# Four graph layers on one core: the third layer's node update contracted in another order, the last layer's loop by eight turns

## The chip, the cores and the metric

The kernel runs on one core of a Trainium2 chip. The metric is the device time of one execution in microseconds (us), the median of several runs. Engines are named as in the profile: PE (TensorE), DVE (VectorE), ACT (ScalarE), POOL (GpSimd) and SP (SyncE, which here only issues DMAs).

## The reference

A network of four graph layers on 3125 nodes (D = 160 features each: CS = 64 scalars and CV = 32 vectors of 3 components) and 103125 edges, all in fp32. Two parts are touched.

The third layer's update: with `x` a node's features and `a` the sums over its edges,

```
u0 = einsum('nu,nv,uvw->nw', xs, a0, Wu_ss)/64 + einsum('nui,nvi,uvw->nw', xv, a1, Wu_vv)*c
u1 = einsum('nu,nvi,uvw->nwi', xs, a1, Wu_sv)*k + einsum('nui,nv,uvw->nwi', xv, a0, Wu_vs)*k
```

The last layer's attention: per edge a message is formed from two node rows, 64 logit features `a` come out of a matrix product, then

```
a = where(a > 0, a, 0.2*a);  a = sum(a * alpha_dot, axis=-1)     # per head, 4 heads of 16
alpha = softmax of a over the edges of a destination node
agg = segment_sum(alpha * h, dst)
```

where `h` is a second product of the same message. The softmax is kept running: a maximum per node is raised and the sums are shrunk as edges come in.

## The kernel before

Every stage is a block in which each engine runs its own program, written out by hand; engines meet through semaphores, and nothing reorders instructions. Within an engine the order of the code is the order of execution.

**The update (stage_layer2, last part).** Nodes are the columns: 10 turns `t` of W = 320 nodes, two turns to a loop iteration. A bilinear term needs the products of every pair `x_u * a_v`. DVE makes them (`prod`, 128x1280 each, L1902): one operand holds rows of `x` broadcast over 32 partitions (`xs4`, `xv4`), the other holds `a` (or `a1`) four times over the partitions. PE contracts each product with a slice of the weights into two PSUM tiles (`p_s`, `p_v`, L1998). A turn has 38 products: 12 for the family Wu_sv, 8 for Wu_ss, 12 for Wu_vs and 6 for Wu_vv. Nine `prod` buffers go round. SP loads the operands for the next turn when DVE has made the last product that reads the single buffer: `xs4` after its 20th product, `xv4` after its 38th. `xs4` and `xv4` are single; `a0` and `a1` are double. ACT loads the weights at the start with 26 DMAs, and DVE scales them before the first operand load may start.

**The last layer's loop (stage_layer3).** Edges are sorted by destination. A turn `u` takes a pair of 128-edge tiles; 428 pairs and three turns of draining give 432 turns, written out `TURN` = 4 to a loop iteration, so 108 iterations. Each of DVE and PE reads its node-block registers with one load at the head of an iteration (`reg_load`). A turn works on three pairs at once:

- for the pair ahead: PE turns one-hots and edge rows (`front_turn`), ACT copies them out of PSUM (`front`, L2480 and L2481, `front_copied`), PE makes the front rows (`front`, L2391 and L2393);
- for the pair `u`: DVE makes the message (L2591) and the first product F; PE turns F in the next turn, ACT copies it (L2509);
- for `prev`: PE makes logits and values (L2430, L2432, `logits_done`), ACT copies 64 logit features (L2518), takes tanh (L2519) and the gate (L2522); DVE applies the leaky rectifier (L2625), multiplies with alpha_dot (L2630) and sums (L2635); DVE makes the second product G;
- for `prev2`: PE turns G (L2444), ACT copies it to `g_t` (L2529), PE makes the heads (L2455, L2457, `heads_done`), DVE weights them (L2656 to L2663), PE sums them per node (L2470, `summed`), and DVE adds the sums (L2594).

DVE's L2596 takes the largest masked logit; PE's next masked product and then its logits wait for it.

## Time and profile before

| | us |
|---|---|
| median of 3 runs | 13256.09 (13255.51 to 13270.1) |
| the profiled execution | 13278.26, its span 13276.5 |
| update: first to last product | 8420.6 to 8955 of the span |
| last layer's loop: first to last message | 9118.5 to 13183.4 of the span |
| busy: PE, DVE, POOL, ACT | 72%, 67%, 57%, 34% of the span |

Times in the rows below are us from the span's start. The update and the loop together are 4600 us, a third of the span; the rest (sorting, the first layers' edges) isn't touched. Busy shares over the whole span mix stages with different limits, so each stage is read by itself.

### The profile page before, as it was taken

How to read it: one execution, taken by the hardware profiler on the slowest of the kernel's cores; microseconds unless marked ns; L12 is line 12 of the kernel's file. 1: busy time of each engine (PE TensorE's matmuls, PEld its weight loads, DVE VectorE, ACT ScalarE, POOL GpSimd, SP SyncE). 2: the span in 40 equal slices, each digit the busy share in tenths (PEclk: the TensorE clock that was granted, in tenths of full speed). 3: DMA queues.
4: the chain of work that ended last, by engine and by line, in shares of the span. 5: the costliest groups of instructions: out<-in, count | busy, mean ns of one | idle time of the engine just before them, and what ended most of it. 6: DMA issues, size and time to landing. Idle time of an engine off the chain costs nothing. (4 is left out here: it accounts for less than half of the span.)

```text
span 13276.5 us, 248283 instructions
## 1 busy us (share of the span) xinstructions
PE 9568.8 (72%) x62786; PEld 6478.2 (49%) x62787; DVE 8841.3 (67%) x26382; ACT 4480.1 (34%) x14978; POOL 7557.1 (57%) x12370
## 2 busy tenths in 40 slices
PE   4444545458888577677766777676888888888887
PEld 2111111136666444444444555335777777777776
DVE  6666766656666433333334555697889989989997
ACT  0000000025555211111112222004777677777775
POOL 2555556555555455555526666003777777777775
PEclk8666666668888777777767788897999999999998
DMA  4000000012222222222213333660000000000000
GB/s 129 22 22 23 23 20 24 17 34 58 58 58 57 54 55 55 55 55 55 55 34 87 81 81 73 115 126 20 21 21 22 21 21 21 21 21 22 21 21 22
DMA packets 901346, 597.92 MB, mean 45 GB/s; under 512 B 654301, under 2 KB 831283, under 8 KB 898584
## 3 DMA queue, kind: packets, MB, share of 16 engines
q0 software_dynamic: 235616, 359.73, 10.8%
q1 hardware_dynamic: 650712, 197.85, 8.3%
q10 hardware_dynamic: 14624, 35.51, 0.7%
q8 instruction: 196, 3.21, 0.1%
q14 instruction: 198, 1.62, 0.0%
HBM read 513.01 MB, written 79.56 MB: 45 GB/s over the span
## 5 line engine op out<-in xcount | busy, mean ns | idle before, releaser
L1290 POOL DMA_INDIRECT l1s_node_rows<-node_table,l1s_edge_rows x1216 | 1245.7, 1024 | 1160.4 <-DMA l1s_edge_rows<-rows_by_src 696.9
L2329 POOL DMA_INDIRECT l_source_rows<-node_table,l_edge_rows x866 | 854.3, 986 | 1102.0 <-DMA l_edge_rows<-rows_by_dst 841.8
L546 PE MATMUL rank<-onehots_and_before,lower_h 128*128 128x427 f16 x812 | 392.4, 483 | 1372.6 <-DVE onehots_and_before L494 651.0
L570 POOL DMA_INDIRECT rows_by_src<-row_s,pos_i x812 | 780.9, 962 | 951.8 <-DVE pos_i L506 686.6
L871 POOL DMA_INDIRECT l_source_rows<-node_table,l_edge_rows x880 | 871.7, 991 | 717.2 <-DMA l_edge_rows<-rows_by_dst 374.5
L1635 POOL DMA_INDIRECT l2s_node_rows<-node_table,l2s_edge_rows x864 | 863.4, 999 | 607.8 <-issue 251.2
L1401 ACT COPY l1s_outer<-l1s_p_outer 128x1024 f32<-128x1024 f32 x304 | 307.6, 1012 | 2053.9 <-remote 1561.0
L570 POOL DMA_INDIRECT rows_by_dst<-row_d,pos_i x812 | 785.1, 967 | 271.4 <-issue 270.5
L1321 DVE TENSOR_TENSOR l_sums_s<-l_sums_s,l1s_p_sums_s 128x8 f32 x1280 | 207.3, 162 | 1089.5 <-remote 688.1
L546 PEld LDWEIGHTS rank<-onehots_and_before,lower_h 128*128 128x128 f16 x812 | 83.2, 103 | 1629.8 <-issue 1121.5
L494 DVE TENSOR_REDUCE onehots_and_before<-onehots_and_before 128x427 f16<-128x2135 f16 x202 | 861.7, 4266 | 22.1 <-issue 20.0
L1375 PE MATMUL l1s_p_outer<-l1s_edge_by_node,l1s_node_rows 128*32 128x128 f32 x7296 | 620.4, 339 | 232.5 <-issue 228.1
L1372 PE MATMUL l1s_p_outer<-l1s_edge_by_node,l1s_node_rows 128*64 128x128 f32 x4864 | 530.1, 333 | 356.1 <-issue 272.1
L939 PE MATMUL l_p_sum<-l_messages,l_node_onehot 128*128 128x384 f32 x1728 | 691.9, 550 | 129.4 <-DVE l_messages L988 84.3
L1665 PE MATMUL l2s_p_sum<-l2s_rows_by_edge,l2s_node_onehot 128*128 128x352 f32 x1728 | 695.0, 520 | 113.8 <-issue 110.3
L548 PE MATMUL rank<-onehots_and_before,ones_h 128*128 128x427 f16 x2030 | 751.7, 484 | 0.0
L1692 DVE TENSOR_TENSOR l_sums<-l_sums,l2s_p_sum 128x512 f32 x440 | 301.2, 684 | 540.2 <-remote 475.1
L1372 PEld LDWEIGHTS l1s_p_outer<-l1s_edge_by_node,l1s_node_rows 128*64 128x64 f32 x4864 | 374.5, 167 | 547.4 <-issue 524.5
L1648 ACT ACTIVATE l2s_rows_by_edge<-l2s_node_rows,l2s_edge_rows 128x160 f32<-128x160 f32 x864 | 293.3, 415 | 1012.8 <-remote 746.2
L2457 PE MATMUL l_p_turn_heads_v<-l_w_hv,l_product_turned 128*128 128x128 f32 x3456 | 573.2, 288 | 0.0
L1375 PEld LDWEIGHTS l1s_p_outer<-l1s_edge_by_node,l1s_node_rows 128*32 128x32 f32 x7296 | 362.8, 132 | 427.5 <-issue 418.0
L1665 PE MATMUL l2s_p_sum<-l2s_node_rows,l2s_node_onehot 128*128 128x160 f32 x1728 | 379.1, 330 | 253.0 <-issue 218.7
(547 smaller groups left out, 29050.1 us busy)
## 6 DMA issues: line engine op xcount, KB each, us to landing
l_xv_by<-h_turned_l SPq DMA_DIRECT2D x120, 320.0 KB
l_source_rows<-node_table,l_edge_rows POOLq DMA_INDIRECT x1746
l_xs_by<-h_turned_l SPq DMA_DIRECT2D x40, 640.0 KB
l1s_edge_rows<-rows_by_src SPq DMA_DIRECT2D x1216, 19.5 KB
l1s_node_rows<-node_table,l1s_edge_rows POOLq DMA_INDIRECT x1216
rows_by_src<-pad_rows_s ACTq DMA_DIRECT2D x16, 1053.0 KB
l2s_edge_rows<-rows_by_src SPq DMA_DIRECT2D x216, 78.0 KB
l_edge_rows<-rows_by_dst SPq DMA_DIRECT2D x220, 72.0 KB
```

Source lines behind the costliest of these rows:

```text
L494: nc.vector.tensor_reduce(hots[:, (r + 1) % 4, SETS, :], hots[:, r, :, :].rearrange("p s b -> p b s"), AX.X, ALU.add).then_inc(counted, 1)
L548: nc.tensor.matmul(to, K["ones_h"][:, :], hots[:, r, m, :], start=False, stop=False)
L570: pool.indirect_dma_start(rows_, bass.IndirectOffsetOnAxis(ap=pos_i[:, k, o, t:t + 1].bitcast(U32), axis=0), tile[:, k, t, :], None).then_ ...
L871: pool.indirect_dma_start(xg[k][:, s, :], None, K["table0"], bass.IndirectOffsetOnAxis(ap=pay[k][:, s, D_SRC:D_SRC + 1].bitcast(U32), axis ...
L939: ins = nc.tensor.matmul(p_sum[:, h, 0:MW], hot[k][:, s, :], msg[k][:, s, :], start=s == PAIR * h, stop=s == PAIR * (h + 1) - 1)
L1290: pool.indirect_dma_start(xg[q][:, s, :], None, table, bass.IndirectOffsetOnAxis(ap=pay[q][:, s, S_DST:S_DST + 1].bitcast(U32), axis=0)).t ...
L1372: nc.tensor.matmul(p_o[rows, q % PO, s, col:col + n], lhs(xg[q][:, s, :]), rhs(eh[q % RING][:, s, :, :]), start=True, stop=True, skip_grou ...
L1375: ins = nc.tensor.matmul(p_o[rows, q % PO, s, col:col + n], lhs(xg[q][:, s, :]), rhs(eh[q % RING][:, s, :, :]), start=True, stop=True, ski ...
L1635: pool.indirect_dma_start(xg[k][:, s, :], None, table, bass.IndirectOffsetOnAxis(ap=pay[k][:, s, S_DST:S_DST + 1].bitcast(U32), axis=0)).t ...
L1665: ins = nc.tensor.matmul(p_sum[:, k % BANKS, h, cols], hot[r][:, s, :], rows[:, s, 0:cols.stop - cols.start], start=s == PAIR * h, stop=s ...
L2329: pool.indirect_dma_start(xg[u][:, s, :], None, K["table0"], bass.IndirectOffsetOnAxis(ap=pay[u][:, s, D_SRC:D_SRC + 1].bitcast(U32), axis ...
L2457: ins = nc.tensor.matmul(p_t[:, s, AT_HV:AT_HV + P], g_t[s][:, (c + 1) * P:(c + 2) * P], w_hv[:, c, :], start=c == 0, stop=c == 1)
```

## The change

**In the update**, the families Wu_sv and Wu_vs are contracted over one index first. For a slice of 16 output features, PE multiplies the weights, laid out by output, with `x` scalars (`hs`, 64 rows) or with `a` scalars (`as_`, a new load), into a PSUM tile `p_mapped` of four banks (`fill`, 4 matmuls, four times in a turn). DVE multiplies that PSUM tile with `a1` or with `x` vectors four times over the partitions (`xf`, a new load), and PE adds up rows with a constant 0/1 matrix (`pick`). The two families so need 6 products each where they needed 12. `p_mapped` is single: a fill waits for the last product that reads it, and the first product after it waits for the fill (`filled`). The order of groups, and with it the point at which SP may load, changes: `xs4` is last read by product 11 of 26, `xv4` by product 23 of 26. Weights come with 16 DMAs.

**In the last layer's loop**, `TURN` is 8, with rings of eight buffers for edge rows, source rows and one-hots (54 iterations of 8 turns). The rectifier is split: leaky(a) = 0.2 a + relu(0.8 a). The linear part comes out of the logits' product as 4 more columns of `w_a`, made beforehand; ACT makes relu(0.8 a) and copies the 4 columns, and DVE keeps one multiplication and one sum, over 17 instead of 16 columns per head. On ACT, the copies of one-hots and edge rows (`front`) stand behind the copies of the turned second product and the exponential.

```diff
-            for g in range(4):
-                groups.append(("v", [("xs4", "a1", lambda k, g=g, i=i: (xs4[:, KB * g:KB * (g + 1), :], a1[k][:, i, :])) for i in range(3)],
-                               [w_sv[:, KB * g + j, :] for j in range(KB)]))
...
+            def mapped(name, w, x, by, g):
+                fills[len(groups)] = [(w[:, KB * g * 4 + 4 * j:KB * g * 4 + 4 * (j + 1), :].rearrange("u w v -> u (w v)"), x) for j in range(KB)]
+                groups.append(("v", [("map", name, lambda k, i=i: (p_m[:, :, 0:W], by[k][:, i, :])) for i in range(3)],
+                               [pick[:, KB * g + j, :] for j in range(KB)]))
+            groups, fills = [], {}
+            of_scalars(0)
+            of_scalars(1)
+            mapped("a1", map_sv, hs, a1, 0)
+            of_scalars(2)
+            of_scalars(3)
+            mapped("a1", map_sv, hs, a1, 1)
+            of_vectors(0)
+            mapped("xf", map_vs, as_, xf, 0)
+            of_vectors(1)
+            mapped("xf", map_vs, as_, xf, 1)
...
+                    if m in fill_first:
+                        dve.wait_ge(filled, t * FILLS + (fill_first.index(m) + 1))
...
+                            sp.dma_start(as_[k][:, :], aT[0:CS, n]).then_inc(arrived_a["lin"][k], 16)
...
+                            for to, of, name in ((a1, aT, "a1"), (xf, hT, "xf")):
+                                for j in range(4):
+                                    sp.dma_start(to[k][j * SPAN:(j + 1) * SPAN, :, :], vectors(of)).then_inc(arrived_a[name][k], 16)
...
+                            def fill(f):
+                                last = first_of[order[f - 1]] + 3 if f else 0
+                                pe.wait_ge(made, t * OPS + (OPS + last))
+                                pe.sem_inc(seen, 1)
+                                for j, (w, x) in enumerate(fills[order[f]]):
+                                    ins = nc.tensor.matmul(p_m[:, j, 0:W], w, x[k][:, :], start=True, stop=True, skip_group_check=True)
+                                ins.then_inc(filled, 1)
...
-    TURN = 4
+    TURN = 8
...
-                            nc.scalar.copy(alphas[:, :, :], logits[:, :, 0:CS]).then_inc(m["alphas_made"], 1)
+                            nc.scalar.activation(alphas[:, :, :, 0:AS], logits[:, :, 0:CS].rearrange("p s (h c) -> p s h c", h=HEADS), ACT.Relu, scale=0.8)
+                            nc.scalar.copy(alphas[:, :, :, AS], logits[:, :, D:D + HEADS]).then_inc(m["alphas_made"], 1)
...
-                            wait("front_turned")
-                            wait("front_done", -1)
-                            front((u + 1) % 4)
                             wait("heads_done", -1)
...
                             nc.scalar.activation(Z[:, :, :, HW - 1], ea[:, :, :], ACT.Exp).then_inc(m["ex_done"], 1)
+                            wait("front_turned")
+                            wait("front_done", -1)
+                            front((u + 1) % TURN)
...
-                            wait("alphas_made")
-                            nc.vector.scalar_tensor_tensor(leaky[:, :, :], alphas[:, :, :], 0.2, alphas[:, :, :], ALU.mult, ALU.max).then_inc(m["leaky_made"], 1)
```

**Where instructions stand, update, PE, before.** The rows are one turn's matmuls into `p_upd_v` and `p_upd_s`; `l_outer` is a product of DVE, and a group of 12 belongs to three products.

```order
L1998 MATMUL l_p_upd_s<-l_h_scalars,l_l_s 64x320
L1998 MATMUL l_p_upd_v<-l_h_vectors,l_l_v 32x320 x3
L2006 REGISTER_ALU
L1998 MATMUL l_p_upd_v<-l_outer,l_w_sv 32x320 x12
...
L1998 MATMUL l_p_upd_s<-l_outer,l_w_ss 64x320 x4
...
L1998 MATMUL l_p_upd_v<-l_outer,l_w_vs 32x320 x12
...
L1998 MATMUL l_p_upd_s<-l_outer,l_w_vv 64x320 x4
```

**The same engine and turn, after the change.** `l_output_of_row` is the 0/1 matrix.

```order
L2029 MATMUL l_p_mapped<-l_h_scalars,l_w_sv_by_output 128x320 x4
...
L2023 MATMUL l_p_upd_s<-l_outer,l_w_ss 64x320 x4
L2039 REGISTER_ALU
L2023 MATMUL l_p_upd_v<-l_outer,l_output_of_row 32x320 x12
L2029 MATMUL l_p_mapped<-l_a_scalars,l_w_vs_by_output 128x320 x4
L2039 REGISTER_ALU
L2023 MATMUL l_p_upd_s<-l_outer,l_w_vv 64x320 x4
```

Eight groups of 12 matmuls have become four, and four fills of 4 matmuls were added. Each fill but the first stands directly behind the group of 12 that ends the reading of the PSUM tile, and four (sv) or three (vv) products of DVE lie between it and the first product that needs it.

**Last layer's loop, ACT, one turn from the logits to the exponentials, before.**

```order
L2518 COPY l_alphas<-l_p_logits_heads_s 128x128
L2519 ACTIVATE l_half_tanh<-l_p_logits_heads_s 128x192
L2522 ACTIVATE l_twice_gate<-l_half_tanh 128x64
L2480 COPY l_onehot_turned<-l_p_front 128x256
L2481 COPY l_edge_rows_turned<-l_p_front 128x128
L2529 COPY l_product_turned<-l_p_turn_heads_v 128x384 x2
L2532 ACTIVATE l_weighted<-l_weight_logits 128x8
L2534 ACTIVATE l_shrink<-l_max_step 128x4
```

**The same stretch after.**

```order
L2562 ACTIVATE l_alphas<-l_p_logits_heads_s 128x8x16
L2563 COPY l_alphas<-l_p_logits_heads_s 128x8
L2564 ACTIVATE l_half_tanh<-l_p_logits_heads_s 128x192
L2567 ACTIVATE l_twice_gate<-l_half_tanh 128x64
L2571 COPY l_product_turned<-l_p_turn_heads_v 128x384 x2
L2574 ACTIVATE l_weighted<-l_weight_logits 128x8
L2524 COPY l_onehot_turned<-l_p_front 128x256
L2525 COPY l_edge_rows_turned<-l_p_front 128x128
L2579 ACTIVATE l_shrink<-l_max_step 128x4
```

One small copy is added ahead of the tanh, and the two `l_p_front` copies now follow the exponential. There is one ACT_TABLE_LOAD in the loop's body in both kernels, at its head. In the built programs, waits and register instructions counted, DVE's body of this loop has 203 instructions before and 390 after; its body of the second layer's loop (L1334), which isn't touched, has 454.

## Rows read from the trace of the kernel before

**Rows 1.** Windows: length, busy (count) of PE, PEld, DVE, ACT, POOL; PE's clock, DMA share, GB/s.

```profile
8420.50:8956.00 535.50, 394.98 (x3120) 174.81 (x3120) 533.68 (x380) 6.71 (x18) 0.00 (x0) 0.95 0.73 135
9118.50:13183.40 4064.90, 3621.22 (x27148) 3038.71 (x27147) 3670.47 (x12931) 2859.77 (x10448) 2997.99 (x7756) 1.00 0.09 21
```

**Rows 2.** Update's groups: busy, mean ns, idle before and what ended it.

```profile
L1902 DVE TENSOR_TENSOR l_outer<-l_xs_by,l_a_four_times 128x1280 f32<-128x1280 f32 x200 | 281.3, 1485 | 20.1 <-DMA l_xs_by<-h_turned_l 19.3
```

**Rows 3.** Timeline of the update: start, us, instruction, idle before it.

```profile
8599.14 9.90 DVE L1902 TENSOR_TENSOR l_outer<-l_xs_by,l_a_four_times 128x1280 f32<-128x1280 f32 x7
...
8626.00 2.35 PE L1998 MATMUL l_p_upd_v<-l_outer,l_w_vs 128*32 128x320 f32 x24 [1.85 <-DVE l_outer L1902]
```

**Rows 4.** DMA from 8400 to 8960: the queue's sum, then issues with KB each.

```profile
q1 hardware_dynamic: 63360, 75.79, 73.7%
l_a_four_times<-sums_turned_l SPq DMA_DIRECT2D x40, 120.0 KB
l_h_scalars<-h_turned_l SPq DMA_DIRECT2D x10, 80.0 KB
```

**Rows 5.** Window in which one turn's `xv4` is loaded, columns as in rows 1.

```profile
8635.00:8654.00 19.00, 13.32 (x112) 5.44 (x110) 19.00 (x15) 0.75 (x2) 0.00 (x0) 0.91 1.09 200
```

**Rows 6.** Timeline of DVE, one turn of the last layer's loop.

```profile
11013.35 0.69 DVE L2596 TENSOR_REDUCE l_pair_max<-l_p_max 128x2 f32<-128x512 f32 x1
...
11017.06 0.42 DVE L2625 SCALAR_TENSOR_TENSOR l_leaky<-l_alphas 128x128 f32<-128x128 f32 x1
11017.40 0.16 DVE L2628 COPY l_maxima<-l_new_max 128x4 f32 x1
...
11019.74 0.36 DVE L2656 TENSOR_TENSOR l_head_spread<-l_p_turn_heads_v,l_axis_kept 128x192 f32<-128x192 f32 x1 [0.40 <-PE l_p_turn_heads_v L2457]
...
11021.09 0.52 DVE L2588 TENSOR_TENSOR l_sums<-l_sums,l_shrink 128x164 f32 x1
...
11022.58 0.69 DVE L2596 TENSOR_REDUCE l_pair_max<-l_p_max 128x2 f32<-128x512 f32 x1
```

**Rows 7.** Timeline of ACT, same turn.

```profile
11016.26 0.27 ACT L2518 COPY l_alphas<-l_p_logits_heads_s 128x128 f32<-128x128 f32 x1 [0.78 <-PE l_p_values_sums L2432]
11016.42 0.34 ACT L2519 ACTIVATE l_half_tanh<-l_p_logits_heads_s 128x192 f32<-128x192 f32 x1
...
11017.01 0.35 ACT L2480 COPY l_onehot_turned<-l_p_front 128x256 f32<-128x256 f32 x1
...
11017.42 0.87 ACT L2529 COPY l_product_turned<-l_p_turn_heads_v 128x384 f32<-128x384 f32 x2
...
11018.79 0.19 ACT L2534 ACTIVATE l_shrink<-l_max_step 128x4 f32<-128x4 f32 x1
```

**Rows 8.** Timeline of PE, same turn.

```profile
11018.06 0.41 PE L2455 MATMUL l_p_logits_heads_s<-l_w_hs,l_product_turned 128*128 128x64 f32 x2 [0.51 <-ACT l_product_turned L2529]
...
11019.56 0.65 PE L2391 MATMUL l_p_front_rows<-l_w_rbf,l_edge_rows_turned 64*128 64x224 f32 x4
```

**Rows 9.** DVE's timeline at the head of an iteration of that loop.

```profile
11002.87 0.33 DVE L2588 TENSOR_TENSOR l_sums<-l_sums,l_shrink 128x164 f32 x1 [0.80 <-issue]
...
11003.75 0.69 DVE L2596 TENSOR_REDUCE l_pair_max<-l_p_max 128x2 f32<-128x512 f32 x1
```

**Rows 10.** By source line, that loop's head: durations ns min/median/max, first and last start.

```profile
L2576 DVEq TENSOR_LOAD <-l_pair_bins x108: 585/590/623, 9113.0 to 13154.5; - x108
L2509 ACT ACT_TABLE_LOAD  x108: 1283/1283/1283, 9115.5 to 13156.0; - x108
```

**Rows 11.** Second layer's loop (L1334): DVE's timeline after its branch at 5109.6.

```profile
5109.57 0.17 DVE L1322 TENSOR_TENSOR l_sums_v<-l_sums_v,l1s_p_sums_v 97x8 f32 x1
5112.74 0.16 DVE L1302 TENSOR_TENSOR l1s_node_in_window<-l1s_edge_rows,l_window_nodes 128x4 f32<-128x4 f32 x1 [3.01 <-issue]
```

**Rows 12.** Instruction fetches (packets, MB) in one iteration of that loop, 5109.7 to 5224.6.

```profile
q14 instruction: 5, 0.04, 0.1%
```

**Rows 13.** DMA, 9305 to 11000, last layer's loop: no instruction queue among its rows.

```profile
q1 hardware_dynamic: 48960, 6.65, 2.6%
```

More of the change, by code:

```diff
@@ L1845, in stage_layer2 @@
             a0, a1 = [sbi(f"a0_four_times{k}", [P, 2, W]) for k in range(2)], [sbi(f"a1_four_times{k}", [P, 3, W]) for k in range(2)]
-            hs, hv = sbi("h_scalars", [CS, W]), sbi("h_vectors", [CV, 3, W])
+            xf = [sbi(f"xv_four_times{k}", [P, 3, W]) for k in range(2)]
+            hs, hv = [sbi(f"h_scalars{k}", [CS, W]) for k in range(2)], [sbi(f"h_vectors{k}", [CV, 3, W]) for k in range(2)]
+            as_ = [sbi(f"a_scalars{k}", [CS, W]) for k in range(2)]
             prod = [sbi(f"outer{m}", [P, KB, W]) for m in range(BUFS)]
@@ L1880, in stage_layer2 @@
             used_for = [freed[x] if x >= 0 else freed[x + OPS] - OPS for x in had]
-            last_use = {g: max(m for m, o in enumerate(ops) if g in o[:2]) + 1 for g in ("xs4", "xv4", "a0", "a1")}
-            loads = {"xs4": 4, "xv4": 12, "a0": 4, "a1": 4, "lin": 2}
-            arrived = {g: semi(f"{g}_in") for g in ("xs4", "xv4", "lin")}
-            arrived_a = {g: [semi(f"{g}_in{k}") for k in range(2)] for g in ("a0", "a1")}
-            made, used, seen, lin_used, upd, upd_copied = (semi(n) for n in ("made", "used", "seen", "lin_used", "upd", "upd_copied"))
+            last_use = {g: max(m for m, o in enumerate(ops) if g in o[:2]) + 1 for g in ("xs4", "xv4")}
+            loads = {"xs4": 4, "xv4": 12, "a0": 4, "a1": 4, "xf": 4, "lin": 3}
+            arrived = {g: semi(f"{g}_in") for g in ("xs4", "xv4")}
+            arrived_a = {g: [semi(f"{g}_in{k}") for k in range(2)] for g in ("a0", "a1", "xf", "lin")}
+            made, used, seen, filled, lin_used, upd, upd_copied = (semi(n) for n in ("made", "used", "seen", "filled", "lin_used", "upd", "upd_copied"))
             T = NP // W
+            fill_first = [first_of[n] for n in order]
             def products(dve, t, k):
@@ L1891, in products @@
                 for m, (g, a, of) in enumerate(ops):
-                    if g not in waited:
+                    if m in fill_first:
+                        dve.wait_ge(filled, t * FILLS + (fill_first.index(m) + 1))
+                        dve.sem_inc(seen, 1)
+                    if g != "map" and g not in waited:
                         dve.wait_ge(arrived[g], t * (16 * loads[g]) + 16 * loads[g])
@@ L1967, in _ @@
                     v = Steps(dve, w_steps)
-                    dve.wait_ge(w_in, 16 * 26)
+                    v.link(nc.vector.memset(pick[:, :, :], 0.0))
+                    for j in range(4):
+                        v.done(nc.vector.memset(free(pick[j * SPAN:(j + 1) * SPAN, 0, j:j + 1], [CV + 4, 8]), 1.0))
+                    dve.wait_ge(w_in, 16 * 16)
                     scaled = lambda ap, f: v.done(nc.vector.tensor_scalar(ap, ap, float(f), None, ALU.mult))
@@ L2016, in _ @@
                                 ins.then_inc(used, len(members))
+                                if n in order[:-1]:
+                                    fill(order.index(n) + 1)
+                            pe.wait_ge(filled, t * FILLS + FILLS)
+                            pe.sem_inc(lin_used, 1)
                             pe.wait_ge(used, t * OPS + 2 * OPS)
@@ L2241, in stage_layer3 @@
             semi = inner.enter_context(Semaphores(nc))
-            four = lambda n, s, d=F32: [sbi(f"{n}{u}", s, d) for u in range(4)]
+            ring = lambda n, s, d=F32: [sbi(f"{n}{u}", s, d) for u in range(TURN)]
             two = lambda n, s, d=F32: [sbi(f"{n}{u}", s, d) for u in range(2)]
-            pay, xg = four("edge_rows", [P, PAIR, SW]), four("source_rows", [P, PAIR, D])
-            hot = four("node_onehot", [P, PAIR, P])
-            hot_t, hot_tb = four("onehot_turned", [P, PAIR * P]), four("onehot_turned_b", [P, PAIR * P], BF16)
+            pay, xg = ring("edge_rows", [P, PAIR, SW]), ring("source_rows", [P, PAIR, D])
+            hot = ring("node_onehot", [P, PAIR, P])
+            hot_t, hot_tb = ring("onehot_turned", [P, PAIR * P]), ring("onehot_turned_b", [P, PAIR * P], BF16)
             pay_t = sbi("edge_rows_turned", [P, P])
@@ L2628, in _ @@
                             nc.vector.tensor_copy(top_b, mn[:, :])
[L2629 to L2630 removed]
+                            wait("alphas_made")
+                            flat = lambda t: t[:, :, :, :].rearrange("p s h c -> p s (h c)")
+                            TT(flat(leaky), flat(alphas), free(alpha_by_head[:, 0, 0:1], [0, PAIR], [1, HEADS * (AS + 1)]), ALU.mult).then_inc(m["leaky_scaled"], 1)
                             wait("spread_made")
```

90 lines of the change are left out of this document (46 added, 44 removed).

## The prediction

> **What bounds the kernel now.** I read the windows by stage first, because the shares of the whole span mix stages. Two stretches are touched. In the update DVE is busy 533.68 of 535.5 us with 380 products [rows 1]; it waits once, 19.3 us for the first load [rows 2]. Seven products take 9.90 us, so one costs 1.41 us, and PE waits for DVE (1.85 us before a group of 12) [rows 3]. DVE is the limit there, with DMA second at a share of 0.73.
>
> The last layer's loop takes 4064.9 us for 431 turns [rows 1], 9.43 us each. DVE is the busiest (3670 us), but the timeline says that it isn't the limit. An ordinary turn is 9.23 us, from L2596 at 11013.35 to the next at 11022.58, and inside it DVE stands 0.40 us before L2656, waiting for PE's heads [rows 6]. PE's heads waited 0.51 us for ACT's copy of the turned product [rows 8]; that copy began at 11017.42, after the two front copies that began at 11017.01 [rows 7]. ACT had waited 0.78 us for the logits, which wait for L2596. So the cycle is L2596, PE's logits, ACT's alphas, tanh, gate, front copies and product copies, PE's heads, DVE's weighting, PE's sums, L2596. The rectifier on DVE lies beside this cycle. At the head of each iteration DVE stands 0.80 us for its branch and register load [rows 9, 10], and ACT loads its table for 1.28 us, once per iteration [rows 10]. Ordinary turns alone would make 431 x 9.23 = 3978 us; the other 87 us are 107 heads at 0.81.
>
> **The update.** DVE: 26 products for 38, 26 x 1.41 = 36.7 us a turn for 53.5. The 12 that read PSUM have no row of their size; below, they cost nothing extra, above, 10% more (0.14 us each, 1.7 a turn). I take 0.05 each, 0.6 in all. The fills: a group of 12 matmuls (24 records, two for each in fp32) takes PE 2.35 us [rows 3], three side by side on 32 columns each, so 4 steps of at most 0.59 us; my estimate for one is 0.53. A fill has 4 matmuls on the full width, 4 such steps, 2.1 us. From the last mapped product to the next fill's end: 2.35 + 2.1 + 0.2 for signals = 4.7 us. DVE has 4 products (5.6 us) to do before the second mapped group, but 3 (4.2 us) before the third and fourth: a wait of 0.5 us twice. The first fill of a turn stands behind the old turn's last group and costs about 0.4. DVE's turn is 36.7 + 0.6 + 1.4 = 38.7 us.
>
> DMA: 75.79 MB in 10 turns [rows 4], 7.58 MB a turn. Added per turn: `xf`, 4 x 120 KB, and `as_`, 80 KB (sizes as of the like loads [rows 4]), 0.57 MB. So 8.15 MB. While loads are under way they move 200 GB/s [rows 5], so a turn needs 40.8 us of DMA, more than DVE's 38.7. Can the queue stay full? Count from the landing of `xv4`, when DVE starts product 15. The `xs4` group was free since product 11, so it is queued; it and `a1`, `xf` take 4.2 MB, 21 us. `xv4` is free after product 23, at 9 x 1.41 + 1 = 14 us, so it is queued before the first are done. The queue never runs dry: the stage becomes bound by DMA at 40.8 us a turn, DVE standing 2 us in each for `xv4`. Start: 10 fewer weight DMAs at about 0.5 us each on ACT's queue, less about 1 us for DVE's larger relayouts, 4 us earlier. From the start of loading (8401.5 before, 8397.5 after) 10 x 40.8 + 2 us to the last `xv4` landing, then 12 products, 18 us: it ends at 8826 where it ended at 8955. **Term: -129 us.** If the DMA rate were better than 200, DVE's 38.7 would hold: -150. If the full queue moved only 190 GB/s: -108.
>
> **The last layer's turn.** On the cycle, the front copies leave the place ahead of the product copies: 11017.42 - 11017.01 = 0.41 us [rows 7]. The rectifier adds to it: the relu is taken at the 0.16 us that the copy L2518 now keeps the next waiting [rows 7], up to 0.04 more; the small copy is like L2534, 0.19 us long, of which about 0.10 to 0.12 holds up the next. I take +0.14. Net 0.27 us earlier. Bounds: 0 (another chain ends as late) and 0.41. Does one? DVE loses L2625, 17.40 - 17.06 = 0.34 us [rows 6], so its own work stands 0.40 + 0.34 - 0.27 = 0.47 us clear of the heads. PE's front L2391 at 11019.56 [rows 8] needs the front copies; these now follow the exponential, itself after the product copies: 11017.42 - 0.27 + 0.87 = 11018.0, 0.2 for the exponential, 0.5 for both copies: 11018.8 with signals, against 11019.3. So it is clear by 0.5 us. **Term: 432 x -0.27 = -117 us.** The Trainium skill (ScalarE: Activation LUTs, "Rules for kernel authors") says to put relu on VectorE, not ScalarE. The trace supports that on this path: the move alone would cost 432 x 0.14 = 60 us, and only the reordered copies pay for it. The forecast holds both; it doesn't change by the rule.
>
> **The iteration head.** 54 heads instead of 108. A plain count gives 54 x 0.81 = 44 us back. But an untouched loop speaks against it. In the second layer's loop, whose DVE body has 454 instructions, DVE stands 3.01 us after the branch, and nothing but issue ends it [rows 11]; in that iteration 5 instruction packets of 8 KB are fetched [rows 12]. With 203 instructions, the last layer's loop fetches none [rows 13]. So a body that is too long is fetched anew each time round. The new DVE body has 390. Five packets for 454 instructions, the fifth perhaps the one behind the loop, put some 90 to 130 in a packet; 390 then touch 4, as the 454 do. I expect the refetch. PE should escape: 8 turns make 8 x 27148 / 432 = 503 matmuls, and the update's loop with 3120 / 5 = 624 ran without a pause that DVE felt [rows 1].
>
> Price of a head then: DVE stands about 3.0 us plus the register load of 0.59 us [rows 10], with 9 registers for 5. That load costs between 0 and 0.59 x 4/5 = 0.47 more; I take 0.25. So DVE reaches L2588 some 3.65 us late. Of this, slack swallows 0.6: between L2588 and L2596 lie 1.49 us in an ordinary turn [rows 6] and 0.88 at a head [rows 9]. The table load falls inside the pause. So 3.05 us a head, 54 x 3.05 = 165, against 87 today. **Term: +78 us.**
>
> **Setup.** Four more ring buffers of each of five kinds are cleared, and five small instructions make the extra columns, about 6 us by the sizes of the tiles at DVE's pace. **+6.**
>
> **Sum.** -129 - 117 + 78 + 6 = -162 us. The profiled execution took 13278.3, so 13116 on its scale; the median of the runs is 22 us lower, 13256.1, which gives **13094 us**.
>
> **Rivals.**
> - **No refetch.** A body of 390 still fits. For it: nothing in this trace lies between 203 and 454. The head then costs about 0.9 (its 0.81 and a little for the registers), 54 x 0.9 = 49 for 165: 13094 - 116 = **12978**. The Trainium skill (Runtime: NRT & Kernel Launch, "Instruction fetch mechanics") gives 32 KiB to such an engine, 512 instructions, in blocks of 256; by that 390 fits. The trace disagrees with it for 454, which was refetched, and shows packets of 8 KB, not 16.
> - **The turn doesn't get shorter.** Something else ends at 9.23: POOL's or DVE's chain, or the front copies. Against: the clearances above. 13094 + 117 = **13211**.
> - **Fills laid bare.** If DVE had to stand the whole 4.7 us four times a turn, the turn is 36.7 + 0.6 + 18.8 = 56 us, the update 20 us slower than now instead of 129 faster: **13243**. Against: three or four products stand between in the built order.
> - **The turn gains the whole 0.41** (ACT's added work hidden): 432 x 0.14 = 60 less, **13034**.
> - **Slower: refetches inside the body too.** If packets came late in the middle of the body, not only at its head, DVE would pause at every one: 4 more a head at 2.6 us, 54 x 10.4 = 562, **13656**. It turns the sign from 1.4 such pauses an iteration on (54 x 2.6 x 1.4 = 197). Against: in the loop that refetches, the pause of 3.01 ended by issue stands at the head [rows 11]; the later packets come while the body runs.
>
> **How the numbers follow.** Forecast 0.58, no refetch 0.14, turn not shorter 0.12, fills bare 0.05, whole 0.41 gained 0.05, slower 0.06. The range goes from the second to the third, with the update's own bounds: 12960 to 13215, which leaves out the last and the bare fills. A measurement here tells 0.2% (27 us) from no change, that is 13230 to 13283. Faster by more: 0.58 + 0.14 + 0.12 + 0.05 = 0.89; within: 0.05; slower: 0.06.
>
> **What the changed profile would show.** Update: products over about 405 us, DMA share near 1, DVE waiting for `xv4` once a turn. Loop: L2596 to L2596 8.96 us in ordinary turns; the front copies behind the exponential; L2656 still waiting for PE; 54 table loads; at each head DVE 3 to 4 us in issue, and 5 or so 8 KB instruction packets per iteration. Wrong if heads stay under 1 us, if ordinary turns stay at 9.23, or if DVE waits on the fills for more than 2 us a turn.

## The result and the profile after

The changed kernel takes 13214.1 us (median of 6 runs, 13188.1 to 13225.5), the kernel before 13264.8 us in the same session (13255.5 to 13273.0): ratio 0.996, 95% interval 0.9947 to 0.9973. It is about 51 us faster, where 162 were forecast. The profiled execution took 13224.4 us against 13278.3.

The windows of the changed kernel, columns as in [rows 1], first the update and then the last layer's loop:

```profile
8417.40:8831.40 414.00, 369.83 (x2456) 183.54 (x2456) 367.24 (x260) 6.71 (x18) 0.00 (x0) 0.96 1.03 188
8980.00:13139.00 4159.00, 3771.09 (x27191) 3094.08 (x27191) 3502.33 (x12517) 2813.38 (x10840) 3012.02 (x7764) 0.98 0.09 21
```

The update went from 534 to 414 us. The loop went the other way: from L2641 (L2596 before) at 8982.1 to the last at 13134.8 are 4152.7 us for 431 turns, 9.635 us each, where it was 9.432. That is 87 us lost out of the 124 that the update gained by its end; the rest of the difference, some 17 us, lies before and behind the loop, where the runs below differ among themselves: the loop's first message maximum (L2641, L2640 in two of them) stands anywhere from 8953 to 9036 in the programs on this chip that have the new update and are nearly equal up to it.

**Update.** The groups of products, in the order operation, count, busy, mean ns, idle before; then the queue's share and bytes:

```profile
L1922 DVE TENSOR_TENSOR l_outer<-l_xs_by,l_a_four_times 128x1280 f32<-128x1280 f32 x80 | 113.8, 1485 | 20.8 <-DMA l_xs_by<-h_turned_l 20.8
L1922 DVE TENSOR_TENSOR l_outer<-l_p_mapped,l_xv_four_times 128x1280 f32<-128x1280 f32 x60 | 85.7, 1484 | 18.4 <-PE l_p_mapped L2029 18.4
L1922 DVE TENSOR_TENSOR l_outer<-l_p_mapped,l_a_four_times 128x1280 f32<-128x1280 f32 x60 | 85.7, 1485 | 28.3 <-PE l_p_mapped L2029 28.3
```

```profile
q1 hardware_dynamic: 65537, 77.85, 102.9%
```

A product that reads PSUM takes 1484 ns, as one from SBUF does (1485). The fills cost DVE 18.4 + 28.3 = 46.7 us in all, 4.7 a turn. They are all that DVE waits for: the 20.8 us for the first load lie ahead of the first product, and no other wait for a load is listed. The DMA engines are busy throughout (share 1.03), and the last packet of `xv4` lands 0.1 to 4.1 us before the product that reads it starts. So DVE's chain, 36.7 + 4.7 = 41.4 us a turn, and the transfers lie close together.

**An ordinary turn of the loop**, DVE, between two heads:

```profile
11013.26 0.69 DVE L2641 TENSOR_REDUCE l_pair_max<-l_p_max 128x2 f32<-128x512 f32 x1 [0.21 <-PE l_p_max L2447]
...
11019.30 0.36 DVE L2700 TENSOR_TENSOR l_head_spread<-l_p_turn_heads_v,l_axis_kept 128x192 f32<-128x192 f32 x1 [0.27 <-PE l_p_turn_heads_v L2501]
...
11021.82 0.32 DVE L2639 TENSOR_TENSOR l_sums<-l_sums,l_p_values_sums 128x164 f32 x1 [0.39 <-PE l_p_values_sums L2514]
11022.35 0.69 DVE L2641 TENSOR_REDUCE l_pair_max<-l_p_max 128x2 f32<-128x512 f32 x1 [0.21 <-PE l_p_max L2447]
```

ACT and PE in the same turn:

```profile
11017.01 0.84 ACT L2571 COPY l_product_turned<-l_p_turn_heads_v 128x384 f32<-128x384 f32 x2
11018.36 0.22 ACT L2574 ACTIVATE l_weighted<-l_weight_logits 128x8 f32<-128x8 f32 x1 [0.52 <-DVE l_weight_logits L2687]
11018.48 0.35 ACT L2524 COPY l_onehot_turned<-l_p_front 128x256 f32<-128x256 f32 x1
11018.73 0.27 ACT L2525 COPY l_edge_rows_turned<-l_p_front 128x128 f32<-128x128 f32 x1
```

```profile
11017.61 0.41 PE L2499 MATMUL l_p_logits_heads_s<-l_w_hs,l_product_turned 128*128 128x64 f32 x2
...
11019.43 0.65 PE L2435 MATMUL l_p_front_rows<-l_w_rbf,l_edge_rows_turned 64*128 64x224 f32 x4 [0.24 <-issue]
```

PE's front in another turn, where the profile names what ended the wait, and, for comparison, ACT's exponential in the turn of [rows 7], of the kernel before:

```profile
9131.47 0.65 PE L2435 MATMUL l_p_front_rows<-l_w_rbf,l_edge_rows_turned 64*128 64x224 f32 x4 [0.48 <-ACT l_edge_rows_turned L2525]
```

```profile
11018.67 0.22 ACT L2532 ACTIVATE l_weighted<-l_weight_logits 128x8 f32<-128x8 f32 x1 [0.38 <-DVE l_weight_logits L2643]
```

The turn is 9.09 us. PE's heads come earlier, 17.61 - 13.26 = 4.35 us after L2641 where they came 4.71 after it [rows 6, 8], and wait for nothing. But ACT now stands 0.52 us for DVE's L2687 before the exponential; the front copies are queued behind that, end at 19.00, and PE's front, which waited for nothing before [rows 8], starts 0.43 us after their end, having stood 0.24; in the other turn it starts 0.42 us after it, and there the wait is put down to L2525. DVE then waits behind it for the sums, 0.39 us, and for the masked maximum, 0.21. The kernel before had already waited 0.38 us at the same exponential.

**A head**, DVE and PE of the changed kernel (the branch stands between L2707 and L2633):

```profile
9131.96 0.69 DVE L2707 TENSOR_TENSOR l_weighted<-l_head_sum,l_weighted 128x96 f32<-128x96 f32 x2
9136.22 0.33 DVE L2633 TENSOR_TENSOR l_sums<-l_sums,l_shrink 128x164 f32 x1 [3.57 <-issue]
```

```profile
9135.48 0.85 PE L2467 MATMUL l_p_turn_heads_v<-ident,l_product 128*128 128x128 f32 x6 [1.12 <-issue]
9137.93 0.58 PE L2445 MATMUL l_p_max<-l_onehot_turned_b,l_apart 128*128 128x512 bf16 x1 [1.60 <-DVE l_pair_max L2641]
...
9139.28 1.06 PE L2476 MATMUL l_p_values_sums<-l_w_v,l_product_turned 128*128 128x128 f32 x4
...
9140.66 0.61 PE L2476 MATMUL l_p_values_sums<-l_w_v,l_product_turned 128*128 128x128 f32 x4
```

Windows of that head and of the turn before it, columns as in [rows 1]:

```profile
9137.90:9140.70 2.80, 2.77 (x12) 2.46 (x13) 2.80 (x11) 0.53 (x2) 1.91 (x5) 0.51 0.00 0
9120.00:9130.00 10.00, 9.38 (x71) 7.78 (x71) 8.90 (x34) 6.89 (x27) 7.19 (x18) 1.00 0.09 21
```

The same 2.8 us behind another head, two iterations later, whose pause was 3.65 us:

```profile
9292.90:9295.70 2.80, 2.74 (x23) 2.60 (x24) 2.80 (x11) 1.10 (x5) 1.91 (x5) 1.00 0.00 0
```

The instruction queue of the whole execution:

```profile
q14 instruction: 466, 3.82, 0.1%
```

DVE stands 3.57 us. The 466 packets are 268 more than the 198 of the same program by four turns (first experiment), 5 for each of 54 iterations less two: the body is fetched anew each time round, as forecast. What wasn't forecast is a second effect. PE stood 1.12 and 1.60 us there, and then its granted clock is 0.51 for 2.8 us, the lower of the two levels (1.2 GHz for 2.4): the same four matmuls of L2476 take 1.06 us, and 0.61 when the clock is back. This doesn't happen at every head: taken over the 6 us behind DVE's pause, the clock is below 0.9 at 29 of the 53 heads inside the loop, and 1.00 at the other 24. The next turn then takes 10.49 us in the median against 9.08, though the pauses are equally long, 3.57 and 3.51 us. What decides between the two isn't shown.

The median turns by position in the iteration are 10.36, 9.46, 9.09, 9.13, 9.09, 9.13, 9.09 and 11.97 us. A head costs 2.9 us in its own turn, 0.8 on average in the next (the clock) and 0.4 in the one after that, over all 4.2 us above ordinary turns (8 x 9.635 less 8 x 9.11).

### The profile page after: what moved, and what is told of

It is laid out like the page before. It is cut to its first block and busy times, and to the rows that moved or that the text cites. A ratio compares the mean times of both kernels' runs of the same rounds, so it can differ in the third digit from the quotient of the medians.

```text
span 13222.2 us, 245568 instructions
## 1 busy us (share of the span) xinstructions
PE 9680.0 (73%) x62146; PEld 6550.0 (50%) x62147; DVE 8506.4 (64%) x25859; ACT 4428.4 (33%) x15356; POOL 7567.9 (57%) x12370
```

## The experiments

Theory 1: the heads are dear because DVE's body of 390 instructions is fetched again, and PE's clock falls behind the pause; the ordinary turn gained 0.12 us and not 0.27 because the front copies behind the exponential are PE's new wait. Rivals: the heads come from the rings of eight, from other engines' longer bodies or from the copies' order; the ordinary turn's gain comes from the rectifier.

"Ordinary turn" is the median, from the trace, of turns that no head touches; "mean" is over the loop. The first eight runs were made on one chip (kernel before beside the first four: 13259.0 us, beside the next four: 13266.5), the last three on another chip, where the kernel before takes 11520.7 us. There the stages ahead of this loop take some 1,750 us less at a higher granted clock, while the loop runs as on the first (9.70 and 9.80 us a turn by eight). So these three are read by their difference in us to the kernel before beside them, and by their loop.

### By four turns

```diff
-    TURN = 8
+    TURN = 4
```

> The changed kernel with the last layer's loop by four turns again (rings of four), all else of the change kept. Theory 1 (VectorE's body of 390 instructions is fetched again at every iteration, the pause costs about 4.3 us a head; a body of some 200 is not fetched again and costs about 0.8 us a head, as in the kernel before): the loop is 432 x 9.11 + 108 x 0.8 = 4022 us against 4162 with eight turns, so about 13075 us (13055 to 13100), with no packets on the instruction queue inside the loop and ordinary turns still 9.1. Rival A (the heads are dear because of the new order of ScalarE's copies, not because of the body's length): heads stay near 3 to 4 us and come twice as often, 432 x 9.11 + 108 x 3.5 = 4314 us of loop, about 13365 us.

Measured: 13054.9 us, ratio 0.9844 (0.982 to 0.9868). Ordinary turn 9.04, mean 9.251. The instruction queue and the register load (by source line, ns min/median/max):

```profile
q14 instruction: 198, 1.62, 0.0%
```

```profile
L2621 DVEq TENSOR_LOAD <-l_pair_bins x108: 585/590/620, 9001.9 to 12965.7; - x108
```

DVE's pause at a head is 0.75 us in the median and a head costs 0.85. Theory 1 holds to 20 us, rival A is out. Rings and the bodies of all engines changed together here; the run "Only VectorE by eight" takes them apart. The longer loop alone takes 13214 - 13055 = 159 us off what the other edits give.

### By six turns

```diff
-    TURN = 8
+    TURN = 6
```

> The changed kernel with the loop by six turns (72 iterations, rings of six, VectorE's body about 295 instructions). Theory 1: a body of that length still stays in place, since ScalarE's 277 and GpSimd's 261 do in the changed kernel, so 432 x 9.11 + 72 x 0.8 = 3993 us of loop, about 13045 us (13025 to 13070), the instruction queue silent. If the limit lies between 277 and 295, the packets are back at each of 72 heads: 72 x 4.27 = 307 us, about 13295 us. Rival (rings longer than four cost time in themselves): slower than the same loop by four turns.

Measured: 13116.1 us, ratio 0.9892 (0.9868 to 0.9916), mean 9.390: neither number. The instruction queue is quiet (199 packets), so 295 instructions stay in place, but a head costs 1.8 us. The register load takes longer than by four or by eight turns (0.84 us there):

```profile
L2621 DVEq TENSOR_LOAD <-l_pair_bins x72: 1032/1348/1641, 8951.1 to 12955.1; - x72
```

In turn it takes about 1.05 and 1.65 us, and DVE stands about 1.35 and 1.93 us. At one of the longer pauses PE stood 1.98 us and its clock fell, as the windows of 6 us from there show (columns as in [rows 1]). The two turns around that head took 10.22 and 11.29 us, those around the head before it, with a shorter pause, 9.64 and 9.70:

```profile
9127.00:9130.00 3.00, 1.77 (x8) 1.41 (x9) 2.57 (x9) 1.50 (x4) 2.44 (x6) 0.74 0.31 67
9130.00:9133.00 3.00, 3.00 (x20) 2.99 (x18) 1.56 (x7) 1.26 (x8) 0.69 (x2) 0.69 0.00 0
```

That pair is the dear kind. Over all heads the clock fell behind 12 of the 36 longer pauses and behind none of the 35 shorter ones. Where it fell, the next turn took 11.2 us on average, and 9.75 where it didn't, as behind a shorter pause. So 0.6 us more of a pause costs 0.6 us as such, and 1.5 us more where the clock falls behind it. Why seven registers load so slowly stays open; it wasn't tried with another offset.

### Front copies at their old place

```diff
+                            wait("front_turned")
+                            wait("front_done", -1)
+                            front((u + 1) % TURN)
                             wait("heads_done", -1)
...
                             nc.scalar.activation(Z[:, :, :, HW - 1], ea[:, :, :], ACT.Exp).then_inc(m["ex_done"], 1)
-                            wait("front_turned")
-                            wait("front_done", -1)
-                            front((u + 1) % TURN)
```

> The changed kernel with the front copies (second turned product) back at their old place, ahead of the copies of the second product; eight turns and the rectifier on ScalarE kept. Theory 1 (the new place of these copies gave VectorE its heads 0.36 us earlier): the ordinary turn goes back to 9.25 from 9.11, with heads as they are, so about 13275 us (13240 to 13310). Rival (the gain of the ordinary turn came from the rectifier's work leaving VectorE alone): ordinary turn 9.11 or less, 13215 us or less; if the copies behind the exponential only delay TensorE's front, even 9.0 and 13165.

Measured: 13347.6 us, ratio 1.0064 (1.0041 to 1.0087). Ordinary turn 9.38, not 9.25, and not below 9.11. PE's heads wait 0.58 us for ACT again, and DVE 0.76 us for the heads:

```profile
11061.78 0.41 PE L2499 MATMUL l_p_logits_heads_s<-l_w_hs,l_product_turned 128*128 128x64 f32 x2 [0.58 <-ACT l_product_turned L2574]
```

The place of these copies is worth 0.27 us. The rectifier on ScalarE, at the old place, costs 9.38 - 9.23 = 0.15; by eight turns, the kernel before has 9.23 too ("The kernel before, by eight turns").

### Front copies in ScalarE's idle time

```diff
                                 nc.scalar.copy(g_t[s][:, :], p_t[:, s, 0:PT]).then_inc(m["g_copied"], 1)
+                            wait("front_turned")
+                            wait("front_done", -1)
+                            front((u + 1) % TURN)
                             wait("ea_made")
                             wait("summed", -1)
                             nc.scalar.activation(Z[:, :, :, HW - 1], ea[:, :, :], ACT.Exp).then_inc(m["ex_done"], 1)
-                            wait("front_turned")
-                            wait("front_done", -1)
-                            front((u + 1) % TURN)
```

> The changed kernel with the front copies between the copies of the second product and the exponential, in the 0.5 to 0.9 us in which ScalarE waits there for VectorE's subtraction. Theory 1 (behind the exponential they are TensorE's new wait, 0.61 us, and VectorE's after it): TensorE's front starts some 0.5 us earlier, the ordinary turn is 8.95 to 9.0 and the time 13145 to 13165 us. Rival (the copies take 0.78 us and push the exponential out by as much as they gain): the ordinary turn is 9.1 to 9.2, 13215 to 13255 us.

Measured: 13144.3 us, ratio 0.9913 (0.9891 to 0.9935), ordinary turn 8.97. ACT and PE of a turn whose L2641 starts at 11052.69:

```profile
11057.42 0.29 ACT L2525 COPY l_edge_rows_turned<-l_p_front 128x128 f32<-128x128 f32 x1
11057.75 0.22 ACT L2577 ACTIVATE l_weighted<-l_weight_logits 128x8 f32<-128x8 f32 x1
```

```profile
11058.54 0.65 PE L2435 MATMUL l_p_front_rows<-l_w_rbf,l_edge_rows_turned 64*128 64x224 f32 x4
```

PE's front starts 5.85 us after L2641 instead of 6.17, straight behind the heads, and the exponential waits no more. Theory 1 holds.

### Rectifier back on VectorE

```diff
-                            nc.scalar.activation(alphas[:, :, :, 0:AS], logits[:, :, 0:CS].rearrange("p s (h c) -> p s h c", h=HEADS), ACT.Relu, scale=0.8)
-                            nc.scalar.copy(alphas[:, :, :, AS], logits[:, :, D:D + HEADS]).then_inc(m["alphas_made"], 1)
+                            nc.scalar.copy(alphas[:, :, :], logits[:, :, 0:CS]).then_inc(m["alphas_made"], 1)
...
+                            nc.vector.scalar_tensor_tensor(leaky[:, :, :], alphas[:, :, :], 0.2, alphas[:, :, :], ALU.mult, ALU.max).then_inc(m["leaky_made"], 1)
```

> The changed kernel with the rectifier back on VectorE (ScalarE copies the logits, VectorE takes the larger of x and 0.2x as before), the new place of the front copies and the eight turns kept. Theory 1 (the move to ScalarE lengthens the path copy of the second turned product to exponential more than it relieves VectorE, as the run with the front copies at their old place suggests: 9.38 us a turn against the 9.23 of the kernel before): the ordinary turn is 8.96 instead of 9.10, about 65 us less, 13150 us (13120 to 13180). Rival (VectorE is the engine that everything waits for, so 0.21 to 0.28 us of work put back on it comes on top): ordinary turn 9.31 to 9.38, 13305 to 13335 us. Neither (one engine's gain is the other's loss): 13215 us.

Measured: 13267.8 us, ratio 1.0005 (0.9991 to 1.002), ordinary turn 9.31. The rival holds: with the copies at the new place, DVE's work is on the cycle, and the exponential waits for it longer, 0.79 us for 0.52:

```profile
11026.36 0.22 ACT L2573 ACTIVATE l_weighted<-l_weight_logits 128x8 f32<-128x8 f32 x1 [0.79 <-DVE l_weight_logits L2687]
```

So neither of the two edits helps the ordinary turn alone: before 9.23, rectifier alone 9.38, copies alone 9.31, both 9.11.

### The update alone

The edit: `stage_layer2` of the changed kernel, `stage_layer3` of the one before.

> The kernel before with the change's update alone (two families contracted first), its last layer untouched. Theory 1: the update's stretch gives 124 us less, as in the trace after, and the last layer's loop stands as before (9.43 us a turn), so about 13140 us (13125 to 13150). Rival (part of the slower loop comes from the update's longer code or its buffers, not from the loop's own edits): above 13170 us, with a loop mean above 9.47.

Measured: 13137.9 us, ratio 0.99 (0.9882 to 0.9919), 129 us less than the kernel before; loop mean 9.446, where it was 9.432. Its ordinary turn is 9.34, though the loop's instructions are those of the kernel before (9.23): by four turns, what a head costs and what an ordinary turn costs can shift by 0.1 us between programs with the same loop, and only the mean compares. Theory 1 holds, and the last layer's edits together cost 13214 - 13138 = 76 us.

### Four turns and copies in the idle time

```diff
-    TURN = 8
+    TURN = 4
```

and the edit of the front copies as in the fourth experiment.

> The changed kernel by four turns, with the front copies between the copies of the second product and the exponential (both edits that helped alone). Theory 1 (heads and ordinary turns add): 0.13 us a turn less than the same kernel by four turns with the copies behind the exponential, 432 x 0.13 = 56 us, about 13000 us (12980 to 13020). Rival (by four turns the heads, where VectorE is late, take back what the earlier front gives): 13040 us or more.

Measured: 13064.5 us, ratio 0.9853 (0.9832 to 0.9873): no gain over four turns alone (loop mean 9.285 for 9.251), so the forecast of 13000 failed. It isn't the heads, which cost 0.4 us, but the ordinary turns, 9.18 us. The loop begins with some turns of 8.93 to 9.05 and then settles at 9.18. The groups of DVE that differ, from 9300 to 13000, first in the fourth experiment's kernel, then here:

```profile
L2660 DVE TENSOR_TENSOR l_dot_parts<-l_weighted_v,l_edge_rows 128x128 f32<-128x128 f32 x390 | 119.9, 307 | 0.0
L2671 DVE COPY l_maxima<-l_new_max 128x4 f32 x390 | 108.2, 278 | 0.0
L2666 DVE TENSOR_TENSOR l_max_step<-l_maxima,l_new_max 128x4 f32<-128x4 f32 x390 | 65.2, 167 | 0.0
```

```profile
L2660 DVE TENSOR_TENSOR l_dot_parts<-l_weighted_v,l_edge_rows 128x128 f32<-128x128 f32 x396 | 257.7, 651 | 0.0
L2671 DVE COPY l_maxima<-l_new_max 128x4 f32 x396 | 184.8, 467 | 0.0
L2666 DVE TENSOR_TENSOR l_max_step<-l_maxima,l_new_max 128x4 f32<-128x4 f32 x396 | 137.6, 347 | 0.0
```

Three instructions take 0.71 us more, and nothing that they wait for is shown; L2662 between them takes 0.13 less (250 ns for 381). GpSimd's first products, again of both kernels:

```profile
11054.65 0.41 POOL L2380 TENSOR_TENSOR l_crossed<-l_weighted_v,l_edge_rows 128x128 f32<-128x128 f32 x1
```

```profile
11018.62 0.41 POOL L2380 TENSOR_TENSOR l_crossed<-l_weighted_v,l_edge_rows 128x128 f32<-128x128 f32 x1
```

The first starts 1.97 us after its turn's L2641, the second 2.55. They run to 3.97 and to 4.61. DVE's L2660 starts at 2.73 and 2.74, so it lies beside some of them in both, but beside the first ones only in the second. GpSimd's next casts wait for DVE's L2679, so a GpSimd that slows DVE is itself made late, and the late phase would keep itself up; that is argued from the order of waits. It gave theory 2: the phase of GpSimd's products against DVE's instructions sets their length.

### The best guess with the rectifier on VectorE

The edits of the last experiment and of "Rectifier back on VectorE" together.

> As the run before it in this list (four turns, front copies between the copies of the second product and the exponential), with the rectifier back on VectorE too. Theory 1 (the rectifier on ScalarE costs 0.15 us a turn in any order of these copies): 65 us less than that run, about 12935 us (12910 to 12960). Rival (with the front copies in ScalarE's idle time the bound is VectorE, and 0.2 us more work on it lengthens the turn): 432 x 0.2 = 86 us more, about 13085 us.

Measured: 13167.5 us, ratio 0.9929 (0.9906 to 0.9952). The rival holds, 103 us more. DVE's L2660 takes up to 0.82 us here.

### Only VectorE by eight

```diff
-    TURN = 8
+    TURN, VTURN = 4, 8
...
-                    with dve.Fori(0, TURNS // TURN) as it:
-                        dve.reg_load(bin_regs, bins[0:1, bass.ds(it * TURN, TURN + 1)])
-                        for u in range(TURN):
+                    with dve.Fori(0, TURNS // VTURN) as it:
+                        dve.reg_load(bin_regs, bins[0:1, bass.ds(it * VTURN, VTURN + 1)])
+                        for u in range(VTURN):
```

> The changed kernel with rings of four and every engine's loop by four turns except VectorE's, which stays by eight: against the run by four turns only the length of VectorE's body differs. Theory 1 (that body alone makes the dear heads): 268 packets more on the instruction queue, a pause of 3.5 us in VectorE's head, about 4.3 us a head 54 times and some 0.4 us at the other engines' heads between, so 13055 - 108 x 0.85 + 54 x 4.3 + 54 x 0.4 = about 13215 us (13190 to 13240). Rival (the longer bodies of TensorE, ScalarE or GpSimd, or the rings of eight, make them): about 13055 us and a quiet instruction queue.

Measured: 11498.1 us for 11520.7, ratio 0.998 (0.9971 to 0.9989), so 23 us less than the kernel before, where four turns throughout gave 204 less: 181 us more. The loop's mean is 9.702 us.

```profile
q14 instruction: 465, 3.80, 0.1%
```

The packets, the turns of 12.0 us and the fallen clock behind them (at 40 of 53 heads) are back with VectorE's body alone. Rings and other engines' bodies are out as the cause. The loss is some 27 us more than forecast; among the iteration's turns the one in the middle, where the other engines have their heads, takes 9.88 us.

### The kernel before, by eight turns

```diff
-    TURN = 4
+    TURN = 8
```

with rings of eight for those of four.

> The kernel before with the eight turns and rings of eight alone (no change of the update, of the copies' order or of the rectifier). Theory 1: the ordinary turn stays at 9.23 to 9.35 us and 108 heads of 0.85 us become 54 of 4.3 us, so 13265 - 92 + 232 = about 13405 us (13380 to 13430), with packets on the instruction queue in each iteration. Rival (the dear heads come from the new order of ScalarE's copies together with the longer loop): heads of 1 us or less, half as many, about 13220 us.

Measured: 11672.4 us, ratio 1.0128 (1.0113 to 1.0144), 152 us more; 468 packets, mean 9.802, ordinary turn 9.23; the clock fell at 48 of 53 heads. Theory 1 holds (140 us expected).

### One gather behind the products

The kernel of "Four turns and copies in the idle time", and in it:

```diff
+                            gather((u + 1) % TURN, it * 16 + 16 * ((u + 1) // TURN + 1), (0,))
-                            gather((u + 1) % TURN, it * 16 + 16 * ((u + 1) // TURN + 1))
                             wait("ux_made", t("ux_made"))
                             cross(v, 0, lambda i, n: uv[:, :, 1, i:i + n, :], pay[u], F[u % 2], "a_crossed")
+                            gather((u + 1) % TURN, it * 16 + 16 * ((u + 1) // TURN + 1), (1,))
```

> The run by four turns with the front copies between the copies of the second product and the exponential (13064 us), with the second of GpSimd's two row gathers issued behind its first five products instead of ahead of them. Theory 2 (that run settled at 9.18 us a turn and not at the 8.97 of the same order by eight turns because GpSimd's products start 2.55 us and not 1.97 us after VectorE's first reduction, and three VectorE instructions that lie beside them take 0.64, 0.35 and 0.48 us instead of 0.30, 0.15 and 0.29): the products now start at about 1.5 us, these three instructions stay short, the ordinary turn is 8.85 to 8.97 us, and the time 13064 - 432 x 0.21 = about 12975 us (12930 to 13000). Rival (the collision is only moved: the gather behind the products delays GpSimd's casts, which VectorE and TensorE wait for): 9.2 us a turn or more, 13065 us or more.

Measured: 11236.0 us, ratio 0.975 (0.9737 to 0.9763), 285 us less than the kernel before; without this edit it was 202 less. Ordinary turn 8.82, mean 9.060. The same three instructions, and L2663 (L2662 there), from 7300 to 11100:

```profile
L2661 DVE TENSOR_TENSOR l_dot_parts<-l_weighted_v,l_edge_rows 128x128 f32<-128x128 f32 x420 | 118.5, 282 | 0.0
L2672 DVE COPY l_maxima<-l_new_max 128x4 f32 x420 | 65.0, 155 | 0.0
L2667 DVE TENSOR_TENSOR l_max_step<-l_maxima,l_new_max 128x4 f32<-128x4 f32 x420 | 63.2, 150 | 0.0
L2663 DVE TENSOR_TENSOR l_new_max<-l_maxima,l_pair_max 128x4 f32<-128x4 f32 x420 | 220.2, 524 | 0.0
```

Theory 2 holds for the three: the edit moved one gather and with it the phase of GpSimd's products, now 1.47 us behind the reduction, and they are short. But the products still lie beside L2661, which takes 282 ns, and L2663 has grown from 250 to 524. So which overlap is dear isn't shown, nor why this turn is 0.15 us below the 8.97 of the fourth experiment. The late gather makes DVE wait 5 us in the whole loop. Its difference to the kernel before is the largest of all runs.

## Why the prediction was right and wrong

The measured time stands at the upper edge of the stated range, and the gain is a third of the one forecast. Two terms of the sum failed, and a third was right in its number only.

**Update, -129: the number right, the wait another one.** The stretch ends 124 us earlier in the trace, and alone it gave 129. The DMA side came out nearly as worked out: 81.5 MB in all, 188 GB/s on average, a turn of 41.4 us for 40.8. But "DVE standing 2 us in each for `xv4`" didn't happen: after the start DVE never waits for a load. It waits for the fills, 4.7 us a turn where 1.4 were forecast, and more than 2 us was a sign named beforehand of being wrong. The third and fourth fill cost 0.9 to 1.0 us each, and a fill takes 2.42 us for 2.1. The first costs 1.8 to 4.2 us in every turn where 0.4 were allowed: PE's four linear matmuls (8 records), 1.4 us, stand ahead of it and were not counted, and in the turns read PE stood 0.8 to 1.3 us before them. DVE's 41.4 us so came near the 40.8 forecast for the transfers. That the total was right is partly luck: cheaper fills would have left DVE waiting for `xv4`, which in three turns lands less than 0.2 us ahead of its first use.

**The turn, -117: the mechanism right, the term mis-sized; measured -52** (432 x 0.12 by turns of 9.11). The step that failed is "PE's front ... is clear by 0.5 us". I let the exponential follow the product copies at once. It waits for DVE's L2687, so the front copies end 5.74 us after L2641 where I had 5.45, and PE starts 0.43 us after their end, for which I had allowed nothing. The first of these waits stood in the trace before: there the exponential already waited 0.38 us for DVE (the line shown above, left out of [rows 7]). With the copies ahead of the exponential, an order other than the one forecast, the turn is 8.97, near the forecast's 8.96. The step on the rectifier was right where it was made: "the move alone would cost" 0.14, and 0.15 was measured at the old place. But it isn't a price that holds in every order. At the new place the same move saves 0.20. The Trainium skill (ScalarE: Activation LUTs, "Rules for kernel authors") puts a rectifier on VectorE; the runs agree at the old place and disagree at the new one.

**The head, +78: the mechanism right, the term mis-sized; measured +140** (54 x 4.2 = 227 for 87). The refetch came with exactly the five packets an iteration. DVE's pause was right too, 3.5 us for 3.65. What failed is the step from DVE's pause to the loop: "slack swallows 0.6 ... so 3.05 us a head". It priced the turn that holds the pause, and rightly (2.9 us measured), and put the turns behind it at nothing. They cost 1.2 us more a head. At 29 of 53 heads PE's granted clock falls to the lower level behind the pause, and there the next turn takes 1.5 us more on average than where it doesn't fall: 43 us in the loop, 0.8 a head. The other 0.4 stand in the second turn behind the head, at either clock; the other kernels by eight turns show 0.0 to 0.2 there, and the cause stays open. Six turns show the fall without any refetch, so it goes with the pause and not with the fetching.

**Setup, +6: not resolved.** From the last product of the update to the loop's first maximum are 164 us before and 151 after, and 149 to 166 in the other runs on this chip. **Sum**: -124 - 52 + 140 and the 17 us outside the loop that point down are -53 us; the profiled executions differ by 54, the medians by 51.

The rivals that I had named weren't the ones that decided. "The turn doesn't get shorter" gave nearly the measured time, 13211 us, but by coincidence: turns did get shorter, and the heads took it back.

## What to carry to other kernels

Count the instructions of a loop's body before unrolling it further: here one engine's step from some 200 to 390 turned 108 cheap heads into 54 dear ones and lost 159 us, though the heads are half as many. Price a pause by what the engines that wait for it lose afterwards, not by its length. In a cycle over four engines, price a move at the place where it will stand, with the waits of the new order; two edits that each cost time made it shorter together, and the next wait was visible in the new timeline as idle time in front of an instruction that others queue behind.

## What the runs showed of the hardware

- An instruction body of 295 on VectorE stays in place; 390 and the 454 of the second layer's loop [rows 11, 12] are fetched again each time, five packets of 8 KB, with a pause of some 2.7 us at the taken branch. The Trainium skill (Runtime: NRT & Kernel Launch, "Instruction fetch mechanics") gives such an engine room for 512 instructions in blocks of 256; by that room alone 390 and 454 would stay, and the traces show otherwise. It also says that a taken branch to a target outside the two blocks held has to wait for a fetch; the trace agrees with a wait at the branch (3.57 us, 0.84 of them the register load), with packets of 8 KB.
- Instructions of VectorE with both inputs in SBUF, and a copy within SBUF, took up to 0.37 us longer in one phase of GpSimd's products than in another: 651 for 282 ns, 347 for 150, 467 for 155, and another one 524 for 250. Nothing in the profile shows it as a wait, and a loop settled in a phase that cost it 0.2 us a turn (9.18 for 8.97). The Trainium skill (GPSIMD Engine Reference, "1. Specifications") says that GpSimd's interface to SBUF is shared with VectorE, with contention for instructions of two inputs in SBUF; the trace agrees for the two with such inputs.
- Loading 5, 7 and 9 registers took 0.59, 1.03 to 1.64 and 0.84 us.
- After PE had stood 1.12 and 1.60 us at a head, it ran at a granted clock of 0.51 for 2.8 us; in the turn before, busy 9.38 of 10 us, at 1.00. Over the 6 us behind DVE's pause the clock was below 0.9 at 29, 35, 27, 46, 40 and 48 of 53 heads with pauses of 3.4 us and more (in the order of the changed kernel, the front copies at their old place, in idle time, the rectifier on VectorE, VectorE alone by eight, the kernel before by eight), at 12 of 36 heads with pauses of about 1.9 us, and at 5 of 677 with shorter ones.
